# Loads moved behind a barrier, and a reordered queue of gathers, sines and a clamp, in a two-layer sequence kernel

## The reference

```
x = x + L1_attn(layernorm(x))            # 16 heads of 8, softmax(q k^T) v, Wo, biases
h = layernorm(x)
# routed block, on h: the 32 tokens of highest weight of each sequence, less the last
weights = h @ router_w + router_b
topv, topi = top_k(weights, 32);  sel = topi[:, :31] (unordered here)
hn = rmsnorm(h[sel], ln1)
q, k = rope(hn @ wq, pos[sel]), rope(hn @ wk, pos[sel]);  v = hn @ wv
a = softmax(q k^T / sqrt(8) + mask[sel][:, sel])
x1 = h[sel] + (a v) @ wo
proc = (x1 + gelu(rmsnorm(x1, ln2) @ w1) @ w2) * weights[sel]
out = x + h * (1 - selected) + scatter(proc)
```

## Time and profile before

| | us |
|---|---|
| median of 3 runs | 1245.72 (1244.88 to 1246.29) |
| the profiled execution's own time | 1249.26 |
| its span (first to last instruction) | 1247.5 |
| PE busy | 1008.7 (81%) |
| DVE busy | 762.7 (61%) |
| ACT busy | 649.8 (52%) |
| POOL busy | 747.0 (60%) |

### The profile page before, as it was taken

One profiled execution on the slowest core, in us unless ns is written; L12 is line 12 of the kernel. 1 busy time (PEld: TensorE's weight loads), 2 busy tenths in 40 slices (PEclk: granted clock), 3 DMA queues, 4 the chain that ended last, 5 costly groups with the idle time before them and its releaser, 6 DMA issues. The chain is left out here.

```text
span 1247.5 us, 30763 instructions
## 1 busy us (share of the span) xinstructions
PE 1008.7 (81%) x9292; PEld 725.2 (58%) x9292; DVE 762.7 (61%) x1580; ACT 649.8 (52%) x1294; POOL 747.0 (60%) x1519
## 2 busy tenths in 40 slices
PE   5588888879979997279999999999999998306165
PEld 4477777669956665156666666666666665104053
DVE  4466666675533433157777777777777775436981
ACT  4356565422223442237777877778777777104112
POOL 3356556537735555456777777777787773571412
PEclk9899999889989999569999999999999999656777
DMA  5700000031123231543344444444444442110000
GB/s 186 275 35 0 0 0 0 2 113 52 52 71 84 80 84 49 151 130 103 108 117 127 126 127 127 119 118 124 128 123 120 118 128 75 42 47 2 0 2 17
DMA packets 92935, 104.82 MB, mean 84 GB/s; under 512 B 11198, under 2 KB 76734, under 8 KB 92490
## 3 DMA queue, kind: packets, MB, share of 16 engines
q1 hardware_dynamic: 85530, 82.73, 23.0%
q0 software_dynamic: 5760, 11.68, 3.0%
q10 hardware_dynamic: 1584, 9.60, 2.0%
HBM read 62.48 MB, written 40.67 MB: 83 GB/s over the span
## 5 line engine op out<-in xcount | busy, mean ns | idle before, releaser
L1287 DVE TENSOR_REDUCE a_neg_max<-a_slot 128x4 f32<-128x1024 f32 x256 | 312.2, 1222 | 133.8 <-PE a_slot L1428 125.5
L1376 ACT ACTIVATE a_pT<-a_slot 128x1024 f32<-128x1024 f32 x256 | 257.7, 1019 | 83.9 <-PE a_slot L1442 79.0
L1442 PE MATMUL a_slot<-a_q_stack,a_k_stack 75*128 75x256 bf16 x1024 | 156.2, 275 | 15.7 <-ACT a_pT L1376 12.0
L1428 PE MATMUL a_slot<-a_k_stack,a_q_stack 72*128 72x256 bf16 x1024 | 158.8, 279 | 7.5 <-DMA a_k_stack<-part_dram 6.6
L1457 PE MATMUL a_ps_o<-a_pT,a_v_pad 128*32 128x256 f32 x2048 | 139.1, 385 | 0.0
L317 DVE TENSOR_TENSOR r_score<-ps_score,r_decay 128x512 f32<-128x512 f32 x128 | 85.0, 687 | 71.8 <-PE ps_score L473 68.4
L1428 PEld LDWEIGHTS a_slot<-a_k_stack,a_q_stack 72*128 72x128 bf16 x1024 | 91.4, 99 | 59.5 <-issue 31.3
L1442 PEld LDWEIGHTS a_slot<-a_q_stack,a_k_stack 75*128 75x128 bf16 x1024 | 92.8, 98 | 52.8 <-DVE a_neg_max L1287 39.1
L689 POOL DMA_INDIRECT y_rows<-m_total,m_token x80 | 76.5, 957 | 66.6 <-ACT m_total L839 52.7
L380 ACT ACTIVATE r_h<-x,r_shift,r_rstd 128x128 f32 (+1 forms) x128 | 56.2, 486 | 80.5 <-POOL r_shift L244 67.8
L682 POOL DMA_INDIRECT sorted_in<-h,m_slot x64 | 63.8, 996 | 34.1 <-issue 18.0
(11 more groups left out here) (293 smaller groups left out, 2312.4 us busy)
## 6 DMA issues: line engine op xcount, KB each, us to landing
a_q_stack<-part_dram SPq DMA_DIRECT2D x64, 288.0 KB
a_k_stack<-part_dram SPq DMA_DIRECT2D x64, 288.0 KB
part_dram<-a_part SPq DMA_DIRECT2D x64, 192.0 KB, 2.7
sorted_in<-h ACTq DMA_DIRECT2D x10, 528.0 KB, 17.3
m_xe<-sorted_in SPq DMA_DIRECT2D x40, 132.0 KB, 2.2
expert_up<-in_eu_dram ACTq DMA_DIRECT2D x1, 4096.0 KB, 14.0
part_dram<-a_part SPq DMA_DIRECT2D x64, 64.0 KB, 2.1
x_rows<-x SPq DMA_DIRECT2D x32, 128.0 KB, 3.5
```

Source lines behind the costliest of these rows:

```text
L1287: nc.vector.tensor_reduce(neg_max[:, p, half, t, g * UNIT:(g + 1) * UNIT], slots[SLOT_OF["m", j]][:], AX.X, ALU.max, negate=True).then_inc ...
L1376: nc.scalar.activation(pT[:, j % PT_RING], slots[SLOT_OF["e", j]][:], ACT.Exp).then_inc(e_read, 1)
L1428: ins = nc.tensor.matmul(slots[SLOT_OF["m", j]][:, q], q_stack[0:QK_ROWS, p, half, head, t * P:(t + 1) * P], k_stack[0:QK_ROWS, p, half, h ...
L1442: ins = nc.tensor.matmul(slots[SLOT_OF["e", j]][:, q], k_stack[0:EXP_ROWS, p, half, head, t * P:(t + 1) * P], q_stack[0:EXP_ROWS, p, half, ...
```

## The change

It makes two groups of edits. At the border of mixture and attention: only the first two of the six loads of `y_rows` stay ahead of the barrier, the other four are issued by SP as its first work behind it; `ones_b` shrinks to 3 x 256 and the DMA broadcasts it over 8 heads; the zeroing of `v_pad` moves from the head of DVE's stream to the end of iterations 0 and 1 of its pipeline, one half of the buffer each; the waits on `preset_v` become waits on a new semaphore `weights_ready`, put where they are needed; and PE's wait for `ones_in` moves to the first `for_exponential`. In the routed phase: POOL's queue becomes 8 gathers of x, 2 of positions, `inv_root(1)`, 4 of positions, `inv_root(2)`, 2 of positions, 8 of mask rows; DVE's clamp moves behind its first `spread_k`; ACT's four sines move between the fourth and the fifth copy of v, with the table of Sin asked for at the phase's start and that of Exp behind the copies of v.

```diff
+EARLY_LOADS = 2
+def load_y(sp, keep, n):
+    some = slice(Y_LOADS[n][0], Y_LOADS[n][-1] + 1)
+    by_tile = keep["y_rows"][NX * P:, :].rearrange("(t p) d -> p t d", p=P)
+    sp.dma_start(keep["h2"][:, some, 0:D], by_tile[:, some]).then_inc(keep["y_loaded"][n], 16)
...
-            for n, tiles in enumerate(Y_LOADS):
-                some = slice(tiles[0], tiles[-1] + 1)
-                sp.dma_start(h2_all[:, some, 0:D], by_tile[:, some]).then_inc(keep["y_loaded"][n], 16)
+            for n in range(EARLY_LOADS):
+                load_y(sp, keep, n)
...
-        ones_b = m.sbuf("a_ones_b", [PARTS, HH, S], BF16)
+        ones_b = m.sbuf("a_ones_b", [PARTS, S], BF16)
...
         def _(sp):
+            for n in range(EARLY_LOADS, len(Y_LOADS)):
+                load_y(sp, keep, n)
             sp.wait_ge(preset, 4)
...
-                    sp.dma_start(k_stack[QK_ROWS:EXP_ROWS, p, half], ones_b[:]).then_inc(ones_in, 16)
+                    sp.dma_start(k_stack[QK_ROWS:EXP_ROWS, p, half], ones_b[:].unsqueeze(1).to_broadcast([PARTS, HH, S])
+                                 ).then_inc(ones_in, 16)
...
             pool.wait_ge(preset, 4)
-            pool.wait_ge(preset_v, 3)
...
             def bias(s, p, r):
+                if isinstance(s, int) and s == 0:
+                    pool.wait_ge(weights_ready, 1)
...
             def pad_v(s, p, r):
+                if isinstance(s, int) and s < 2:
+                    pool.wait_ge(preset_v, 2 * (s + 1))
...
         def _(dve):
-            nc.vector.memset(v_pad[:], 0.0).then_inc(preset_v, 1)
-            dve.wait_ge(preset_v, 1)
-            nc.vector.memset(v_pad[:, :, :, :, AD:AD + 1], 1.0).then_inc(preset_v, 1)
             dve.wait_ge(bias_sum, 1)
...
+            def preset_v_pad(s, p, r):
+                if not (isinstance(s, int) and s < 2):
+                    return
+                nc.vector.memset(v_pad[:, s], 0.0).then_inc(preset_v, 1)
+                dve.wait_ge(preset_v, 2 * s + 1)
+                nc.vector.memset(v_pad[:, s, :, :, AD:AD + 1], 1.0).then_inc(preset_v, 1)
...
-            pe.wait_ge(preset_v, 3)
-            pe.wait_ge(ones_in, 16 * 2 * HALVES)
+            pe.wait_ge(weights_ready, 1)
...
+                    if j == 0 and isinstance(s, int) and s == 0:
+                        pe.wait_ge(ones_in, 16 * 2 * HALVES)
...
-            gather(lambda g: pos[:, g:g + 1], w["d_position"], rows_ids, pos_in)
+            positions(range(0, 2))
             inv_root(1)
+            positions(range(2, 6))
+            inv_root(2)
+            positions(range(6, G))
             gather(lambda g: mask_rows[:, g], w["d_mask"], rows_ids, mask_in)
-            inv_root(2)
...
-            dve.wait_ge(mask_in, 16 * G)
-            v.tensor_scalar(mask_rows, mask_rows, -3.0e38, None, ALU.max).then_inc(clamped, 1)
...
-            for g in by_dve:
+            for n, g in enumerate(by_dve):
+                if n == 1:
+                    dve.wait_ge(mask_in, 16 * G)
+                    v.tensor_scalar(mask_rows, mask_rows, -3.0e38, None, ALU.max).then_inc(clamped, 1)
                 spread_k(v, dve, g, k_spread_dve)
...
         def _(act):
+            nc.scalar.preload_act_table(ACT.Sin)
...
             for g in range(G):
+                if g == HG:
+                    act.wait_ge(angle_done, 1)
+                    for u in range(2):
+                        nc.scalar.activation(cos[:, :, u], angle_c[:], ACT.Sin)
+                    nc.scalar.activation(sin[:, :, 0], angle[:], ACT.Sin, scale=-1.0)
+                    nc.scalar.activation(sin[:, :, 1], angle[:], ACT.Sin).then_inc(rope_ready, 1)
                 act.wait_ge(qkv_done, g + 1)
...
-            act.wait_ge(angle_done, 1)
-            for u in range(2):
-                nc.scalar.activation(cos[:, :, u], angle_c[:], ACT.Sin)
-            nc.scalar.activation(sin[:, :, 0], angle[:], ACT.Sin, scale=-1.0)
-            nc.scalar.activation(sin[:, :, 1], angle[:], ACT.Sin).then_inc(rope_ready, 1)
+            nc.scalar.preload_act_table(ACT.Exp)
```

More of the change, by code:

```diff
@@ L659, in _ @@
                 sp.wait_ge(s, 16 * NX // RING)
-            by_tile = y_rows[NX * P:, :].rearrange("(t p) d -> p t d", p=P)
-            for n, tiles in enumerate(Y_LOADS):
-                some = slice(tiles[0], tiles[-1] + 1)
-                sp.dma_start(h2_all[:, some, 0:D], by_tile[:, some]).then_inc(keep["y_loaded"][n], 16)
+            for n in range(EARLY_LOADS):
+                load_y(sp, keep, n)
             for s in xe_loaded:
@@ L1054, in attention_phase @@
         preset_v = m.sem("a_preset_v")
+        weights_ready = m.sem("a_weights_ready")
         ones_in = m.sem("a_ones_in")
@@ L1263, in _ @@
             nc.vector.tensor_copy(ident_b[:], ident[:])
-            nc.vector.tensor_scalar(bq_scaled[:], bq[:], SCALE, None, ALU.mult).then_inc(preset_v, 1)
+            nc.vector.tensor_scalar(bq_scaled[:], bq[:], SCALE, None, ALU.mult).then_inc(weights_ready, 1)
+            def preset_v_pad(s, p, r):
[4 more added lines that the diff above has]
+                nc.vector.memset(v_pad[:, s, :, :, AD:AD + 1], 1.0).then_inc(preset_v, 1)
             def given_added(s, p, r):
@@ L1332, in _ @@
                            (maximum(3), 3), (moments3, 6), (moments, 0), (maximum(4), 3), (normalise(1), 5),
-                           (maximum(5), 3), (add_up, 8), (maximum(6), 3), (maximum(7), 3)], B, ROUNDS)
+                           (maximum(5), 3), (add_up, 8), (maximum(6), 3), (maximum(7), 3), (preset_v_pad, 0)], B, ROUNDS)
         @block.scalar
         def _(act):
-            act.wait_ge(preset_v, 3)
+            act.wait_ge(weights_ready, 1)
             nc.scalar.preload_act_table(ACT.Exp)
@@ L1723, in _, with gather, positions @@
             index = lambda a, g: bass.IndirectOffsetOnAxis(ap=a[:, g:g + 1], axis=0)
-            def gather(to, table, at, done):
-                for g in range(G):
+            def gather(to, table, at, done, groups=range(G)):
+                for g in groups:
                     nc.gpsimd.indirect_dma_start(to(g), None, table, index(at, g)).then_inc(done, 16)
+            def positions(groups):
+                gather(lambda g: pos[:, g:g + 1], w["d_position"], rows_ids, pos_in, groups)
             def inv_root(n):
```

## The result

The changed kernel takes 1229.22 us (median of 4 runs, 1228.40 to 1233.32), against 1246.01 us (1244.88 to 1247.15) for the kernel before, timed beside it on one chip. The ratio is 0.9872, with a 95% interval from 0.9848 to 0.9896: a gain of about 16 us, some 13 to 19. The forecast was a gain of 22.7 us and a time of 1223.0 us. The sign was right; the size was not: the time lies at the very end of the stated range, 1218.5 to 1230, and the forecast ratio, 0.982, lies outside the interval. The profiled execution of the changed kernel took 1228.4 us, with a span of 1226.6 us.

The account below looks back on a forecast made before the run. TensorE bounds the attention's loop, so gains come from the way in and the routed phase, where POOL's queue is the bound. 6.8 + 3.0 + 12.9 = 22.7 us, taking the median from 1245.72 to 1223.0; range 1218.5 to 1230.

Parts of the forecast that it names:

- The barrier: Between mixture and attention: four loads leave its front, so it opens 6.8 us earlier (5.5 to 7.2).
- Rival (b): Fixed work such as clearing semaphores or code fetch sets the barrier's opening; gain 15.9 us, time 1229.8; chance 0.07.
- The head: Start of the attention: first fill issued about 19 us behind the opening instead of 22.0; gain 3.0 us (0 to 4.6).
- rival (a): SP's queue, held until the bulk drains, takes the head's whole gain; total gain 19.2 us, time 1226.5; chance 0.10.
- The loop: Attention's PE-bound loop: no edit touches it, all engines shift together; gain 0.
- The routed phase: POOL's order, sines and clamp together: 10.7 + 3.9 - 1.7 = 12.9 us gained (10.5 to 14.5).
- POOL's order: Routed phase: 1/rms no longer behind eight gathers, so `d_xn` starts 10.7 us earlier.
- The sines: Routed phase: table load leaves the chain, rope starts 14.55 us earlier, 3.9 more than `d_xn`.
- The slack of 1.3 us: Routed phase: angles end at 1117.8, ahead of the fourth v copy at 1119.1; each us later beyond it costs one.
- The clamp: Routed phase: behind the first spread it is on the path, giving back 1.7 us on PE's mask chain and DVE's spreads.
- One sign of being wrong: Routed phase: `d_xn` still waiting for POOL by over 1 us would show the prediction wrong.
- rival (c): Attention loop: TensorE's clock rises later, making the kernel slower; two iterations of full-clock work done low give 1256; chance 0.03.

Follow-up runs that it names:

- Group 1: Against the kernel before: itself unchanged, ratio 1.0000; only the loads moved, 1.0046; only the attention's head edits, 0.9946; only the routed phase's edits, 0.9920.
- early5: Changed kernel with five loads ahead of the barrier instead of two, only load 5 behind it; ratio 0.9857 to the kernel before.
- drain_mid: Changed kernel with one more POOL drain ahead of the last 10 of 40 pairs of scatters; ratio 0.9862 to the kernel before.
- best_a: Changed kernel with four loads ahead of the barrier, clamp ahead of the first spread, extra POOL drains at steps 0 and 24; 1222.14 us, ratio 0.9803 to the kernel before.
- first pair: Profile of the kernel before shown ahead of the prediction, against the changed kernel's first profile; stretches sum to 747.20 and 726.83 us, gain 20.4.
- loads_only: Kernel before with only loads 2 to 5 moved behind the barrier, PE still waiting early for the ones; ratio 1.0046 to the kernel before.
- clamp_first: Changed kernel with the clamp ahead of DVE's first spread instead of behind it; ratio 0.9858 to the kernel before.
- best_b: Changed kernel with five loads ahead of the barrier, clamp first, an extra POOL drain ahead of the scatters of y; 1224.98 us, ratio 0.9827 to the kernel before.
- second pair: Kernel before and changed kernel, each profiled again, on two other chips; stretches sum to 743.81 and 726.65 us, gain 17.2.
- best_c: Changed kernel with five loads ahead of the barrier and the clamp ahead of the first spread; 1225.92 us, ratio 0.9839 to the kernel before.

## Why the prediction was right and wrong

**The barrier, 6.8 forecast, 1.8 to 2.9 measured: wrong.** The step that failed is "with 1.65 us as before from SP's last issue to the opening, it opens at about 500.15". It held for the kernel before, where SP was last, and was carried to one where SP no longer is. The prediction asked what could be late instead and answered that POOL had ended at 496.21. That is the end of its last counted instruction; its drain isn't counted as busy, and ended at 502.84 in the very trace that was read. The row of the opening shows only an idle gap put down to `POOLq L92`; the piece that stays was there to be read (the lines of L90 above), on POOL's queue at the block's last line. Rival (b), work behind the last scatter that another thing sets, had the mechanism in part. It gave the barrier nothing, when 2.9 us lay free between the end of POOL's drain (502.84) and SP's arrival (505.7). Group 1 shows that the loads bring that opening alone; `early5` shows that SP doesn't set it; `drain_mid` and `best_a` move it by changing the drain. Moving SP could win only the distance to the second arrival, 2.9 us, and that is what the first pair shows.

**The head, 3.0 forecast, 3.2 to 3.8 measured: right.** Each of its steps came within 0.4 us: transpose at 4.6 (4.8), `split_qk` at 8.8 (9.0), fill at 18.7 (19), and 17.27 (17.4) without the bulk. Its reason was right in part. The prediction let the stores land late behind the bulk, and held that the issues just fit. In the changed kernel it was the other way: the stores were first issued 2.7 us late, since SP was held for 6.45 us by a copy of ones, and then took no longer to land than in `early5`. That is rival (a)'s mechanism, at a price of 1.3 to 1.9 us instead of all the head's gain, and that the number came out is in part luck. (The four loads' issue, put at 6.7 us, is 6.8 by the numbers given there; nothing hangs on it.) The Trainium skill, page "DMA: Bandwidth & Descriptors", section "Queues, rings and completion order", has the descriptors of one issuer taken in ring order. The traces agree with that where the bulk ended late: in `loads_only` PE's wait for the ones ended 0.4 us behind the last load's landing (545.8), and in `clamp_first`, where the bulk landed 18.4 us behind the opening, the first fill came 2.6 us behind the last store's issue instead of 1.5. They show besides that the issuer itself stands still.

**The loop, 0 forecast, 0.8 to 0.9 measured.** The nine profiles of kernels with the head's edits show 540.55 to 542.98 us there (`best_a`'s 545.72 apart), those without them 541.69 to 542.96. It can't be told from the spread, and no mechanism was looked for.

**The routed phase, 12.9 forecast, 11.4 to 12.8 measured: right, a little high.** POOL's order gave 11.0 to 11.1 (10.7 forecast). One gather beside DVE's `d_xn` took 1.96 us and one beside its product for the mean square 1.43, against 0.94. The mask gathers, which the prediction let stretch as well, took 0.95 us each, the last one 1.08. The sines were to give 3.9 and gave 2.7 to 3.7. The slack of 1.3 us that was to lie between the angles and the fourth copy of v was minus 1.0. The last positions were issued 1.2 us later than worked out (by 1105.80, 3.4 us behind `d_xn`'s start, for 2.15) and the angles ended 8.4 us behind it instead of 6.95, while the fourth copy ended 7.4 behind it instead of 8.27. The 8.27 belonged to the first profile's clock, as its second profile shows. The clamp took 1.6 (1.7), as worked out. One sign of being wrong was badly chosen: `d_xn` did wait over 1 us for POOL (2.34), but the prediction's own times already had it wait that long (from 1108.5 to 1110.85).

**TensorE's clock, rival (c), 0.03.** It did not come: in the changed kernel and in `best_a` and `best_b` full clock was granted some 45 us behind the opening, and some 48 before. Of these, only `best_a` had a lower clock again while PE was still busy, at the loop's other end.

**The base.** The sum was made against one profile and subtracted from the median of runs. That was harmless for the loads and POOL's order, but the barrier and the sines were read from stretches that were 1.1 and 1.0 us longer than in the second profile. By the first pair the total missed only 2.3 us, and by luck: 3.9 were lost at the barrier, and 1.7 came unforeseen from head and loop. By the second pair, whose 17.2 us stand nearest to the timed gain, the forecast missed 5.5 us: 5.0 at the barrier and 1.5 in the routed phase, less 1.0 that head and loop gave beyond it.

## What to carry to other kernels

Before a wait is priced as gone, list every queue's arrival at it, with the instructions that a profile doesn't count as busy; the second to arrive is what the change can win up to. A drain behind many indirect DMAs is such an arrival, and a drain placed earlier, where POOL waits anyway and can catch up, can shorten the one at the barrier. A bulk transfer that is moved in front of small ones can stop the issuing queue itself, so keep only the last large load behind the barrier (`early5`), or issue the small ones first (not tried here).

## What the runs showed of the hardware

POOL's drain at a block's end grows with the indirect DMAs ahead of it, but not with all of them. Its end, counted from the start of the last scatter ahead of it, was 3.05 us with 20 scatters since the last drain, 3.65 with 32, 4.90 with 48 (the drain at step 24 of `best_a`), 5.97 with 60 (the added drain of `drain_mid`), 6.27 with 64 (`best_a`'s drain at step 0, behind the scatters of the sort), 7.59 with 80 and 7.57 with 144. These are good to 0.05 us. The 60 leave out the 64 scatters of the sort, which in `drain_mid` lay behind the last drain as well, and which came ahead of a pause of about 15 us. By the equal times of 80 and 144, and by 5.97 for 60 + 64, these 64 did not count. From 32 to 80 that is 0.08 us for each. A pause alone doesn't explain it: in the routed phase of the changed kernel 24 gathers went out by 1116, nothing for 96 us, then 8 scatters, the last of them here, with the drain behind it:

```profile
1221.60 0.95 POOL L1772 DMA_INDIRECT out_dram<-d_square,d_rows  x1 [0.30 <-issue]
...
L90 POOLq DRAIN  x1: 9784/9784/9784, 1215.5 to 1215.5; - x1
```

It ended 3.65 us behind that scatter, like the 32 scatters of `best_a` that came without such a pause. Why the sort's scatters don't count is open, and what the drain does for each was not tried.

SP's issue of a DMA behind the large loads is held, twice in most executions: load 5 when it followed load 4 at once took 2.8 to 4.3 us, where the others took under 0.9, and the first copy of ones 1.9 to 7.1, where the other three took 0.6 to 0.8. In the ten profiles in which loads 4 and 5 went out together, that copy's issue ended 9.4 to 10.3 us behind the start of load 5's, whether it had begun 6 to 8 us behind it (1.9 to 3.6 us of hold) or 2.9 to 3.9 (5.5 to 7.1). So a copy that is ready earlier is held longer: what was left of the bulk seems to set the moment. With load 5 behind the barrier and load 4 ahead of it (`early5`, `best_b`, `best_c`) load 5 took 0.7 and the copy ended 6.6 to 7.2 behind its start.

Two profiles of one unchanged kernel differed by 3.4 us from the last scatter on, where the interval of its ratio to itself over 12 runs is 0.17%, or 2.2 us, to each side. Chips differed by some 20 us ahead of the barrier, nearly all of it in the scatters of the sort.
